# Which TensorE results release the eight scatters of a batch

## The reference

```python
topk_idx, topk_w = _route(x, gate_weight, e_bias)      # 8 experts per token
flat_e = topk_idx.reshape(-1)
order = jnp.argsort(flat_e)
sorted_e = flat_e[order]
pos = jnp.arange(Sk) - offsets[sorted_e]                # place of the row in its expert
tok_sorted = x[order // K]
xe = jnp.zeros((E, CAP, H), x.dtype).at[sorted_e, pos].set(tok_sorted, mode='drop')
h = jax.nn.silu(jnp.einsum('ech,efh->ecf', xe, w1)) * jnp.einsum('ech,efh->ecf', xe, w3)
ye = jnp.einsum('ecf,ehf->ech', h, w2)
```

## Time and profile before

| | us |
|---|---|
| median of 3 runs | 2098.22 (2096.67 to 2100.63) |
| profiled execution, its time | 2083.96 |
| span of its trace | 2082.2 |
| first attention layer, steady part | 113.66 to 885.24 |
| TensorE busy in the span | 1805.8 (87%) |
| VectorE busy in the span | 1473.8 (71%) |
| ScalarE busy in the span | 1104.8 (53%) |
| GpSimd busy in the span | 889.5 (43%) |

### The profile page before, as it was taken

One profiled execution on the slowest core, in us unless ns is written; L12 is line 12 of the kernel. 1 busy time (PEld: TensorE's weight loads), 2 busy tenths in 40 slices (PEclk: granted clock), 3 DMA queues, 4 the chain that ended last, 5 costly groups with the idle time before them and its releaser, 6 DMA issues.

```text
span 2082.2 us, 55906 instructions
## 1 busy us (share of the span) xinstructions
PE 1805.8 (87%) x20848; PEld 1442.2 (69%) x20848; DVE 1473.8 (71%) x5299; ACT 1104.8 (53%) x2283; POOL 889.5 (43%) x884
## 2 busy tenths in 40 slices
PE   5998989888889888963999996999999999987855
PEld 3777777777777777752888884777777777753334
DVE  5788888888878888864444444666666666667988
ACT  2555545555555555521222224666666666657875
POOL 1255555555555555555777773111111111111137
PEclk8999999999999999985999998999999999998989
DMA  9822111122111111124999983111111111102355
GB/s 238 225 83 59 54 51 38 50 63 62 44 35 44 44 43 34 29 64 133 211 213 218 222 162 74 45 48 40 48 45 42 48 40 48 40 25 92 152 193 211
DMA packets 184172, 187.93 MB, mean 90 GB/s; under 512 B 37042, under 2 KB 166613, under 8 KB 181856
## 3 DMA queue, kind: packets, MB, share of 16 engines
q1 hardware_dynamic: 136384, 142.69, 22.0%
q0 software_dynamic: 47520, 41.67, 10.8%
HBM read 103.72 MB, written 140.77 MB: 117 GB/s over the span
## 4 chain that ended last, share of the span: by engine, by line
PE 58%; DVE 14%; another core or an unknown queue 8%; issue 8%; DMA 5%; POOL 4%; ACT 3%; SPq 1%; POOLq 0%; ACTq 0%; DVEq 0%
PE bank L431 8%; PE bank L396 7%; PE tiles L349 7%; PE bank L446 6%; PE bank L514 5%; PE tiles L366 5%; DMA accumulator<-ye,tid 4%; PE bank L477 3%; PE bank L466 3%; DVE hmax L1612 2%; PE tiles L1251 2%; PE tiles L333 2%; POOL accumulator L1413 2%; DVE h_ring L1605 2%
## 5 line engine op out<-in xcount | busy, mean ns | idle before, releaser
L1887 POOL DMA_INDIRECT expert_rows<-pay,idx x512 | 504.6, 986 | 370.0 <-issue 129.8
L794 DVE TENSOR_REDUCE mt<-tiles 128x16 f32<-128x2048 f32 x128 | 293.5, 2293 | 108.4 <-PE tiles L349 96.9
L595 ACT ACTIVATE pt<-tiles 128x2048 f32<-128x2048 f32 x128 | 241.5, 1887 | 12.6 <-PE tiles L366 7.9
L1413 POOL DMA_INDIRECT accumulator<-ye,tid x128 | 198.1, 1548 | 91.7 <-issue 34.0
L1903 POOL TENSOR_TENSOR rstd<-var,minus_half 128x2 f32<-128x2 f32 x70 | 49.1, 701 | 424.7 <-DVE var L871 424.5
L618 ACT ACTIVATE qkp<-bank,kb,keep 128x128 f32<-128x128 f32 x500 | 206.3, 479 | 0.0
L431 PE MATMUL bank<-xt,w_q 128*128 128x128 f32 x1024 | 168.4, 288 | 3.2 <-issue 2.3
L396 PE MATMUL bank<-pt,vx 128*32 128x128 f32 x4096 | 158.1, 276 | 9.9 <-issue 7.5
L615 ACT ACTIVATE qkp<-bank,qb 128x128 f32<-128x128 f32 x256 | 97.2, 381 | 127.9 <-PE bank L431 127.6
L349 PE MATMUL tiles<-qkp 32*128 32x256 f32 x2048 | 156.2, 404 | 8.7 <-issue 5.4
L431 PEld LDWEIGHTS bank<-xt,w_q 128*128 128x128 f32 x1024 | 139.2, 197 | 27.5 <-issue 25.5
(11 more groups left out here) (256 smaller groups left out, 3997.3 us busy)
## 6 DMA issues: line engine op xcount, KB each, us to landing
expert_rows<-zt POOLq DMA_DIRECT2D x16, 1032.0 KB
xr<-expert_rows SPq DMA_DIRECT2D x64, 258.0 KB
cxax<-in_ctx SPq DMA_DIRECT2D x128, 128.0 KB
cxax<-accumulator SPq DMA_DIRECT2D x128, 128.0 KB, 2.3
hidden_away<-h_ring SPq DMA_DIRECT2D x8, 1536.0 KB, 5.0
res<-in_x SPq DMA_DIRECT2D x64, 128.0 KB
accumulator<-xa SPq DMA_DIRECT2D x64, 128.0 KB
accumulator<-zt SPq DMA_DIRECT2D x64, 128.0 KB
```

Source lines behind the costliest of these rows:

```text
L595: nc.scalar.activation(pt[r % 2][:, :, :], tiles[:, :, :], ACT.Exp).then_inc(sem(sm("exp_done")), 1)
L794: nc.vector.tensor_reduce(mt[:, :].rearrange("p (i n c) -> p i n c", i=RT, n=2 * KC)[:, :, :, 0], tiles[:, :, :].rearrange("p i (n k) -> p ...
L1413: nc.gpsimd.indirect_dma_start(out=acc[p][:, :], out_offset=bass.IndirectOffsetOnAxis(ap=tid[r][:, h:h + 1], axis=0), in_=ye[r][:, h, :], ...
L1887: G.indirect_dma_start(out=xe[:, :], out_offset=bass.IndirectOffsetOnAxis(ap=idx[r][:, n:n + 1], axis=0), in_=pay[r][:, :], in_offset=None ...
```

## The change

The eight waits of a batch get other semaphores. The first five scatters wait for the transposed scores (`scores_t`) of batch b + 5, which are made in slot b + 6; all five have the same condition, so nothing separates them once it holds. The last three wait for the scores (`scores`) of batch b + 7, made at the head of slot b + 7. Number, order, data and addresses of the scatters are the same.

```diff
@@ -1880,8 +1880,7 @@
                     return
                 b, r = k
                 pool.wait_ge(sem("slot_step_0"), 3 * b + 3)
-                steps = (("qk_done_0", ahead(b, 7)), ("o_done_0", ahead(b, 4)), ("up_done_0", ahead(b, 3)), ("pv_done_0", ahead(b, 5)),
-                         ("s_done_0", ahead(b, 7)), ("down_done_0", ahead(b, 3)), ("v_done_0", ahead(b, 8)), ("st_done_0", ahead(b, 6)))
+                steps = 5 * (("st_done_0", ahead(b, 5)),) + 3 * (("s_done_0", ahead(b, 7)),)
                 for n in range(TOPK):
                     pool.wait_ge(sem(steps[n][0]), steps[n][1])
                     G.indirect_dma_start(out=xe[:, :], out_offset=bass.IndirectOffsetOnAxis(ap=idx[r][:, n:n + 1], axis=0),
```

## The result

The changed kernel takes 2185.49 us (median of 4, 2181.70 to 2186.53) against 2099.43 us of the kernel before in the same session: **ratio 1.0397, 95% interval 1.0358 to 1.0436.** Later the same pair gave 1.0387 (1.0347 to 1.0427). The forecast was 2180 us and slower.

A forecast was written before the change was run, and what follows sets the result against it. No engine was full; TensorE's larger groups were taken to report about 1.7 us after a run's last scatter start. Cases of 15.66 and 12.80 us gave 15.25 us a slot, +82 us on 2098.22: 2180 us, eight-in-ten range 2043 to 2225.

The forecast's parts named there:

- That results of TensorE are held behind the last start of a run: While scatters follow one another, TensorE's larger groups report late, about 1.7 us after the last scatter has started.
- Part one: Three scatters behind the scores: transposed scores reported 4.75 us into the slot instead of 6.07, gaining 1.32 us a slot.
- Part two: Five scatters behind the transposed scores: reports come free 7.54 us behind those; two cases, weighted to 15.25 us a slot.
- case one: Behind the five scatters, query/key projections and output are held too: 15.66 us a slot, 1.88 more; taken six in seven.
- case two: Projections and output get through the five; up projection, logits, values and scores are held: 12.80 us a slot, 0.98 less.
- the rest: The layer's start and its end from 885 us, outside the 56 slots: 0, with 5 us to either side.
- the upper bound: Over 56 slots, +1.88 us each, +105 us, with a further 20 us if the hold is 2.39 us.
- The faster rival: Projections get through the run or the hold leaks between scatters: 12.8 us a slot likeliest, 2043 us; chance 0.33.
- Nothing happens: The 2.4 us come from something all slots with routing have, not the scatters: 13.78 us a slot, 2098 us; chance 0.09.

The follow-up runs named there:

- g2_five: Kernel before with five scatters behind the transposed scores, the other three waiting as before: 2286.75 us against 2100.38 us.
- f2_add: Changed kernel with each scatter replaced by an addition on GpSimd and no DMA: 2014.21 us; kernel before 2099.33 us.
- h1_oob: Changed kernel with the scatters' bound set to row 0, so practically no row is written: 2144.27 us; kernel before 2101.80 us.
- the first group: Four runs beside a kernel before of 1942.92 us: no scatters 1924.34, three behind scores 1938.51, five behind transposed scores 1945.80, changed order without rows 1951.18 us.
- part one alone: Kernel before with three scatters behind the scores, the other five waiting as before: 1938.51 us (before 1942.92) and 2116.92 us (before 2100.38).
- e4_oob: Changed kernel with the scatters' bound set to row 0, practically no row written: 1951.18 us; kernel before 1942.92 us.

## Why the prediction was right, and where it was not

**That results of TensorE are held behind the last start of a run** proved true of holding sessions: 1.70 us behind the last start for the pair of g2_five, and 2.03, 2.11, 2.07, 2.11, 2.18 and 1.88 us behind runs of three to five or more in the slots shown; the prediction had 1.71. It takes an indirect DMA (f2_add), the bytes of its rows don't matter (h1_oob), and there are sessions without it (the first group). The last was in none of my rivals.

**Part one** was forecast to bring 1.32 us a slot. The transposed scores came at 5.3 instead of the forecast's 4.75 us, and alone the part costs 0.4 us a slot against the profile of before (0.3 by the 16.5 us of its session). The failed step took one lucky case for the rule: there the last of the three had started 3.33 us into the slot just the same, but the report came 1.42 us behind it, not 2.0. And it forgot that the first of the three joins on to the scatter before. Only beside the five does part one pay.

**Part two, the choice of case.** I gave case one (projections and output held) six in seven. It is not what happens: in the usual slot L615 and L819 came at 7.6 us, right behind their predecessors, which my text had named as the sign of the *faster* case. Reports that fell into the first 1.5 us or so of a run got through (L819 at 752.86, first start at 751.37), the next, due at 754.47, did not.

**Part two, the size of case two.** It was 12.80 us, and the slot from 745.29 has 15.37. Term by term, forecast and measured:

| from | to | forecast | measured |
|---|---|---|---|
| transposed scores (L670) | first of the five | 0.71 | 751.37 - 750.60 = 0.77 |
| first | last of the five | 5.12 | 756.48 - 751.37 = 5.11 |
| last start | logits (L689) | 1.71 | 758.59 - 756.48 = 2.11 |
| logits | L937 | 0.50 | 759.12 - 758.59 = 0.53 |
| L937 | next maxima (L794) | 1.10 | 760.66 - 759.12 = 1.54 |
| maxima | transposed scores | 3.66 | 750.60 - 745.29 = 5.31 |
| sum | | 12.80 | 15.37 |

(The last row is of the same slot's start.) The largest miss, 1.65 us, is the last row: it stood there as if nothing were held, although three scatters behind the scores were the very thing of part one, which my own text put at 4.75. The next two, 0.44 and 0.40, are the values and scores made only behind the hold, partly at the lower clock, and the longer hold. Case one would by the same corrections have come to over 17 us. So 15.25 against 15.32 us is **the wrong case with terms that were too small**, two errors that cancel, and no proof of the reasoning. The total is luck as well: "the rest" was put at 0, with 5 us to either side, and the profiled pair has 16 us there, which the median of the kernel before, 14 us above its profile, makes good again.

Two smaller slips changed nothing. A scatter takes 0.986 us on GpSimd and not 0.975; the sum used the 1.28 us between starts. And a hold of 2.39 instead of 1.71 us would add 0.68 x 56 = 38 us, not 20, to the upper bound.

**Left out altogether** were TensorE's own stop and the lower clock behind it; the clock alone is some 0.43 us a slot.

**The faster rival** had the right picture of who gets through and the wrong price. **Nothing happens** is what free sessions come near to: 1945.80 and 1951.18 against 1942.92 us for part two and for the whole order without rows.

The rule of the Trainium skill that I weighed (SBUF — State Buffer, Who interferes with whom) sees the engines' ports apart from the DMAs' and lets only VectorE and GpSimd get in each other's way. f2_add agrees on that pair (0.62 instead of 0.16 us), the free session agrees on TensorE, and 15.32 against 12.85 us a slot in holding sessions does not. Whether ports are what is shared there no run tells.

**Open.** What sets a session's kind: chip and program don't, as one chip ran the kernel before in 2099.33 us and later in 1940.45; what else was running beside it is not on record. Why a report comes free 2.1 us behind the last start, what path it shares with an indirect DMA, and whether it is GpSimd's issuing or the packets. No order beat the kernel before in a holding session with all its scatters; in a free one part one alone was 4.4 us faster in a single run, 0.2%, no more than the measurement tells.

## What to carry to other kernels

Indirect DMAs from GpSimd beside a busy TensorE can make its results late without any wait in the program: look for "remote" in front of the engines that read them, and measure from the last start of a run. What counts is which result falls behind the run, so move scatters only with the whole slot drawn up, and close each cycle of a forecast with the same held results that its other parts use. Compare also the cycles in which the clock never fell: they tell a wait from what the clock adds to it. Before an effect without a named releaser is designed around, run the unchanged kernel in several sessions: here 155 us lay between the two kinds.

## What the runs showed of the hardware

- The same kernel on the same chip took 2099.33 and 1940.45 us in two sessions. Where the difference lies is seen from part one alone, which ran in both kinds: 11.53 against 14.18 us a slot, 56 x 2.65 = 148 of the 2116.92 - 1938.51 = 178 us, while GpSimd's own time for a scatter is the same (0.985 and 0.986 us).
- While reports are held TensorE goes on for some 1.5 us past the first held result (754.47 to 756.03), then stops: behind 26 of the 32 products of the values in the slot shown, behind 15 to 26 in the others that have a stop, behind 28 in the slot of g2_five.
- After such stops its granted clock fell to the 1.2 GHz level for a while, and the scores behind took 1.72 us (changed kernel) and 2.09 us (g2_five) instead of 1.15.
- An indirect DMA with a list of 64 rows costs GpSimd 0.917 us, with 128 rows 0.985. With all rows out of bounds its packets are still there (47520 in the software queue, as before), and it costs 0.986 (e4_oob).
